# Linear attention on one core: keys turned by VectorE in 32x32 blocks and carried through device memory, in place of turns on TensorE

## What is computed

```python
x = L0_attn_x
n = layernorm(x)
q, k = phi(n @ Wq.T + bq), phi(n @ Wk.T + bk)      # phi = elu + 1, 16 heads of 32
v = n @ Wv.T + bv
# for each token t, with sums over the tokens up to t of the same sequence:
kv = sum(k[s] outer v[s]);  ksum = sum(k[s])
o[t] = (q[t] @ kv) / (q[t] . ksum + 1e-6)
x = x + o @ Wo.T + bo
x = x + experts(layernorm(x))                      # kept only where counts <= cap
```

## Time and profile before

| | us |
|---|---|
| median of 3 executions | 2012.27 (2009.82 to 2013.5) |
| the profiled execution | 2015.74 |
| its span, first to last instruction | 2013.9 |

### The profile page before, as it was taken

One profiled execution on the slowest core, in us unless ns is written; L12 is line 12 of the kernel. 1 busy time (PEld: TensorE's weight loads), 2 busy tenths in 40 slices (PEclk: granted clock), 3 DMA queues, 4 the chain that ended last, 5 costly groups with the idle time before them and its releaser, 6 DMA issues.

```text
span 2013.9 us, 60872 instructions
## 1 busy us (share of the span) xinstructions
PE 1968.6 (98%) x25932; PEld 1731.4 (86%) x25932; DVE 1524.1 (76%) x3260; ACT 737.3 (37%) x1419; POOL 899.6 (45%) x982
## 2 busy tenths in 40 slices
PE   6899999999999999999999999999999999999997
PEld 5788888888888888888888888888888888888886
DVE  4777777777778877777777877777777797777776
ACT  3333343333433333333333433333333333333332
POOL 3454434545345545345545344544345444355421
PEclk8999999999999999999999999999999999999999
DMA  5221222212222212222212222212222122222111
GB/s 178 64 74 65 85 77 94 86 58 82 85 75 94 87 44 90 91 75 91 90 44 85 90 81 85 77 63 85 84 87 86 59 80 86 75 95 86 44 38 49
DMA packets 87391, 159.28 MB, mean 79 GB/s; under 512 B 15313, under 2 KB 15313, under 8 KB 87121
## 3 DMA queue, kind: packets, MB, share of 16 engines
q1 hardware_dynamic: 84720, 154.83, 22.8%
q10 hardware_dynamic: 2400, 0.55, 0.1%
HBM read 121.66 MB, written 33.68 MB: 77 GB/s over the span
## 4 chain that ended last, share of the span: by engine, by line
PE 91%; DVE 6%; issue 1%; ACT 1%; POOL 1%; DMA 0%; SPq 0%; DVEq 0%; POOLq 0%
PE ring L598 35%; PE ring L612 33%; PE num_ps L700 6%; PE ring L663 6%; PE num_ps L686 3%; PE ring L674 3%; PE num_ps L712 2%; DVE s_mask L867 2%; DVE den L1104 1%; PE ring L635 1%; PE ring L648 1%; DVE rden L1111 1%; DVE v_tok L897 1%; DVE o_lo L1100 1%; ACT o_hi L834 0%
## 5 line engine op out<-in xcount | busy, mean ns | idle before, releaser
L1180 POOL TENSOR_TENSOR k_sum<-k_sum,q_raw 128x512 f32<-128x512 f32 x128 | 164.6, 1286 | 596.2 <-DVE q_raw L878 596.2
L780 ACT ACTIVATE e_tmp<-ring,bias_n 128x512 f32<-128x512 f32 x256 | 176.1, 688 | 396.7 <-PE ring L598 396.7
L867 DVE TENSOR_TENSOR s_mask<-ring,causal 128x512 f32<-128x512 f32 x512 | 315.1, 678 | 0.0
L612 PE MATMUL ring<-wv_hi,xt_hi 128*128 128x260 f32 x1024 | 301.0, 294 | 3.1 <-DVE gate_x L899 2.3
L612 PE MATMUL ring<-wo_hi,o_hi 128*128 128x260 f32 x1024 | 288.2, 281 | 3.2 <-DVE o_lo L1100 1.9
L612 PE MATMUL ring<-wo_hi,o_lo 128*128 128x260 f32 x1024 | 290.7, 284 | 0.0
L612 PE MATMUL ring<-wv_hi,xt_lo 128*128 128x260 f32 x1024 | 289.1, 282 | 0.0
L612 PE MATMUL ring<-wv_lo,xt_hi 128*128 128x260 f32 x1024 | 288.9, 282 | 0.0
L612 PE MATMUL ring<-wo_lo,o_hi 128*128 128x260 f32 x1024 | 288.7, 282 | 0.0
L878 DVE SCALAR_TENSOR_TENSOR k_t<-ring,bias,e_tmp 128x512 f32<-128x512 f32 x128 | 96.2, 751 | 197.1 <-ACT e_tmp L782 194.3
L598 PE MATMUL ring<-xt_hi,wk_hi 128*128 128x512 f32 x512 | 215.8, 421 | 7.4 <-DVE wk_lo L322 5.6
(11 more groups left out here) (145 smaller groups left out, 4211.3 us busy)
## 6 DMA issues: line engine op xcount, KB each, us to landing
x_tok<-in_x SPq DMA_DIRECT2D x128, 256.0 KB, 3.8
res<-in_x SPq DMA_DIRECT2D x128, 256.0 KB, 2.7
out<-res SPq DMA_DIRECT2D x128, 256.0 KB, 2.0
x_in<-in_x_t SPq DMA_DIRECT2D x124, 256.0 KB, 4.6
x_rows<-moments_rows SPq DMA_DIRECT2D x31, 512.0 KB, 3.7
k_t<-in_wk_t SPq DMA_DIRECT2D x1, 1024.0 KB, 9.7
q_raw<-in_wq_t SPq DMA_DIRECT2D x1, 1024.0 KB, 11.8
v_tok<-in_wv_t SPq DMA_DIRECT2D x1, 1024.0 KB, 13.9
```

The costliest lines, as they stand in the source:

```text
L612: mm = pe.matmul(bank[:, 0:HW], rows[a](k), w[b][:, k, h, :], start=n == 0, stop=n == 3 * KD - 1)
L780: act.activation(e_tmp[:, m], bank, ACT.Relu, bias=bias_n[:, m, g:g + 1], scale=-1.0).then_inc(phi_relu.handle, 1)
L867: dve.tensor_tensor(s_mask[:, j], ring[:, st.bank(u)].rearrange("p (g t) -> p g t", g=KD), repeat(causal, KD), ALU.mult).then_inc(free[st. ...
L1180: pool.tensor_tensor(k_sum[:, g], k_sum[:, g], q_raw[:, g], ALU.mult).then_inc(prod.handle, 1)
```

## The change

The four transposes on PE and the copy by ACT go. DVE turns a tile's keys with one instruction that transposes each 32x32 block in place of its own (`turn_keys`, now in DVE's program) into a new buffer `k_turned`. The blocks still have to change places between groups of 32 partitions: SP writes `k_turned` (256 KB) to a buffer in device memory (`send_keys`) and reads it back with four transfers, one for each 32 partitions of the target (`fetch_keys`), in pieces of 128 elements, into one of two buffers `k_tok`. PE's `add_state` waits for the four. Tile 1's keys are turned at the start of tile 0 in DVE's order, tile 2's at the start of tile 1, tile 3's at c = 2 behind the chunk V0, and tile 0's of the next block at c = 3 behind `xt_lo` of tiles 0 and 1; each in front of that tile's phi or `o_lo`. The last tile of every second block isn't turned any more, because its state isn't used; before it was.

The ring loses its four "T" uses, so a block has 48 places in place of 54. The constant `spread` is made smaller, to find room, and is set by four copies on 32 partitions in place of one.

```diff
-SKIPS = {0: 1, 1: 1, 3: 3}
+SKIPS = {0: 1, 3: 2}
...
-        uses += [("T", c)] + chunk_uses(c, 0, 1)
+        uses += chunk_uses(c, 0, 1)
...
+        def send_keys(b, c):
+            if (b, c) not in KEY_TILES:
+                return
+            n = KEY_TILES.index((b, c))
+            sp.wait_ge(keys_turned.handle, n + 1)
+            if n > 1:
+                sp.wait_ge(keys_in[n % 2].handle, 16 * HPG * (n // 2))
+            sp.dma_start(keys_dram[n % 2], k_turned).then_inc(keys_out.handle, 16)
+
+        def fetch_keys(b, c):
+            if (b, c) not in KEY_TILES:
+                return
+            n = KEY_TILES.index((b, c))
+            sp.wait_ge(keys_out.handle, 16 * (n + 1))
+            if n > 1:
+                before, tile = KEY_TILES[n - 2]
+                sp.wait_ge(summed.handle, TPB * before + tile + 1)
+            heads = keys_dram[n % 2].rearrange("(i a) j x -> j a i x", i=HPG)
+            for j in range(HPG):
+                sp.dma_start(k_tok[j * HD:(j + 1) * HD, n % 2].rearrange("a i g b -> a i (g b)"), heads[j]
+                             ).then_inc(keys_in[n % 2].handle, 16)
...
-                if c == 0 and st.has("turn"):
-                    load_x(st)
-                    load_features(st)
+                if c == 0:
+                    send_keys(t, 1)
+                    if st.has("turn"):
+                        load_x(st)
+                    fetch_keys(t, 1)
+                    if st.has("turn"):
+                        load_features(st)
+                if c == 1:
+                    send_keys(t, 2)
...
+                if c == 1:
+                    fetch_keys(t, 2)
+                if c == 2:
+                    send_keys(t, 3)
+                    fetch_keys(t, 3)
+                if last and st.has("proj"):
+                    send_keys(t + 1, 0)
+                    fetch_keys(t + 1, 0)
...
-            for g in range(KD):
-                mm = pe.transpose(bank[:, g * P:(g + 1) * P], k_t[:, st.off % 2, g, c * P:(c + 1) * P], ident)
-            mm.then_inc(full[st.bank(u)].handle, 1)
...
-            pe.wait_ge(free[st.bank(("T", c))].handle, st.freed(("T", c)))
+            n = KEY_TILES.index((st.off, c))
+            pe.wait_ge(keys_in[n % 2].handle, 16 * HPG * (n // 2 + 1))
...
-                if attn:
-                    u = ("T", c)
-                    act.wait_ge(full[st.bank(u)].handle, st.filled(u))
-                    act.activation(k_tok, ring[:, st.bank(u)], ACT.Copy).then_inc(free[st.bank(u)].handle, 1)
...
+        def turn_keys(b, c):
+            if (b, c) not in KEY_TILES:
+                return
+            n = KEY_TILES.index((b, c))
+            if n:
+                dve.wait_ge(keys_out.handle, 16 * n)
+            dve.transpose(k_turned.rearrange("p j (g b) -> p g j b", g=KD),
+                          k_t[:, b % 2, :, c * P:(c + 1) * P].rearrange("p g (j a) -> p g j a", j=HPG)
+                          ).then_inc(keys_turned.handle, 1)
...
+                if c < 2 and attn:
+                    turn_keys(st.off, c + 1)
...
+                if c == 2 and attn:
+                    turn_keys(st.off, 3)
+                if last and proj:
+                    turn_keys(st.off + 1, 0)
```

More of the change, by code:

```diff
@@ L76, in ring_uses_alone @@
 def ring_uses_alone():
-    uses = [("T", 0)]
+    uses = []
     for c in range(TPB):
         if c < TPB - 1:
-            uses += scores_of(c + 1) + [("T", c + 1)]
+            uses += scores_of(c + 1)
         uses += [("O", (c, 0)), ("O", (c, 1))]
@@ L88 @@
 BANK_ALONE = {**{("S", (c, j)): j for c in range(1, TPB) for j in range(HPG)},
-              **{("T", c): HPG for c in range(TPB)},
-              **{("O", (c, h)): HPG + 1 - h for c in range(TPB) for h in range(2)}}
+              **{("O", (c, h)): HPG + h for c in range(TPB) for h in range(2)}}
 assert len(USES) % NBANK == 0
@@ L96, in part_of @@
         return "proj" if place[0] == 0 else "attn"
-    return "attn" if kind in ("T", "O") else "proj"
+    return "attn" if kind == "O" else "proj"
 def uses_of(parts):
@@ L184, in attention @@
     moments_dram = nc.dram_tensor("moments_rows", (2, P, TPB, 2), F32, kind="Internal").ap()
+    keys_dram = nc.dram_tensor("keys_turned", (2, P, TPB, P), F32, kind="Internal").ap()
+    KEY_TILES = [(b, c) for b in range(n_blocks) for c in range(TPB) if b % 2 == 0 or c < TPB - 1]
     out_t = io["out"].rearrange("(n p) d -> n p d", p=P)
@@ L227, in attention @@
     head_cols = sb("head_cols", [P, 2, HD])
-    spread = sb("spread", [P, 2, KD, P], F32R)
+    spread = sb("spread", [P, 2, P], F32R)
     bias = sb("bias", [P, 2, KD])
@@ L340, in set_from_constants @@
         dve.wait_ge(const_set.handle, CONSTS)
-        dve.tensor_copy(spread, spread_f).then_inc(bias_set.handle, 1)
+        for g in range(KD):
+            rows = slice(g * HD, (g + 1) * HD)
+            dve.tensor_copy(spread[rows], spread_f[rows, :, g]).then_inc(bias_set.handle, 1)
         dve.tensor_reduce(lo_rows, low.rearrange("p s g j -> p (s g j)"), AXX, ALU.add
                           ).then_inc(bias_set.handle, 1)
-        dve.wait_ge(bias_set.handle, BIASES + 2)
+        dve.wait_ge(bias_set.handle, BIASES + KD + 1)
     def set_gates(dve):
@@ L435, in attention @@
     summed = sem("summed")
+    keys_turned, keys_out = sem("keys_turned"), sem("keys_out")
+    keys_in = [sem(f"keys_in{n}") for n in range(2)]
     kv_summed, kv_kept = sem("kv_summed"), sem("kv_kept")
@@ L647, in spread_reciprocals @@
                     k, rows = BANK[("R", g)], slice(g * HD, (g + 1) * HD)
-                    mm = pe.matmul(ring[:, k, s * BT // 2:(s + 1) * BT // 2], spread[rows, s, g, :], rden[rows],
+                    mm = pe.matmul(ring[:, k, s * BT // 2:(s + 1) * BT // 2], spread[rows, s], rden[rows],
                                    start=True, stop=True, skip_group_check=True, tile_position=(g * HD, 0))
@@ L711, in add_state @@
                     cols = slice((g * HPG + j) * HD, (g * HPG + j + 1) * HD)
-                    pe.matmul(kv_ps[j * HD:(j + 1) * HD, g * HD:(g + 1) * HD], k_tok[:, cols], v_tok[:, c, cols],
+                    pe.matmul(kv_ps[j * HD:(j + 1) * HD, g * HD:(g + 1) * HD], k_tok[:, n % 2, j, g], v_tok[:, c, cols],
                                    start=first_tile(st, c) and g == 0, stop=g == KD - 1, skip_group_check=True,
@@ L723, in body @@
                 last = c == TPB - 1
-                if attn and (proj or c == 0):
-                    turn_keys(st, c)
                 if c == 1 and not attn:
@@ L749, in body @@
                     chunks(st, c, 2, 3)
-                if not proj and not last:
-                    turn_keys(st, c + 1)
                 if attn:
```

11 lines of the change are left out of this document (5 added, 6 removed).

## The result

The changed kernel takes 1964.09 us (median of four executions, 1961.08 to 1965.99); the kernel before, in executions beside it, 2012.88. The ratio is 0.9757 [0.9739, 0.9776]: 48.8 us less, where 51.1 were forecast; the median lies in the range, 1952 to 1985, and in the likelier 1954 to 1968. The profiled execution took 1966.0 us (span 1964.2), where the sum gave 1964.6.

A forecast was written before the change was run, and what follows sets the result against it. PE's distances from start to start were taken to bound all blocks but first and last. -52.0 saved on PE, +0.6 and +0.3 at the start give -51.1: 1961.2 us median, range 1952 to 1985, likely 1954 to 1968.

The forecast's parts named there:

- PE saves per block: Four sets of transposes and three changes of matmul kind leave PE: 0.42 + 0.43 + 0.43 + 0.41 = 1.69 us.
- DVE's transpose: Each new 128x512 transpose on DVE takes 0.69 us, like the statistics instruction; range 0.35 to 3.4.
- slack before the block's first K matmul: DVE's last `xt_lo` of tile 3 ends at 996.74, PE is free for K matmuls at 997.26: 0.52 us.
- a transpose at which the pace of before returns: In tile 3 a DVE transpose of 1.28 + 1.69 = 3.0 us uses up the whole gain per block.
- slack of tile 0's keys: Store, four loads and landing take 8.8 us of a 12.0 us budget before `add_state`: 3.2 us left.
- The first half of the question: What the turns cost PE, as distances from start to start: 1.69 us per block, 52.4 over 31 blocks.
- the prediction's 52.0: PE's whole saving: 52.4 us over 31 blocks, less 0.4 at the first block's tile 0, where PE waits for DVE.
- Rival (C): PE is bound by something unseen, such as weight loading; the freed 1.7 us per block become wider distances: 2012; chance 0.03.
- Rival (A): DVE's transpose is slow, tile 3's pace passes to DVE from 1.28 us; chance 0.05 for 1970 to 2005, 0.05 slower.
- The keys' way: Tile 0's keys through memory: store 0.3 and 2.0, four issues 1.86, landing 4.6, together 8.8 us; hidden, costing nothing.
- The end: Last block: two tiles wait for keys, against ACT's copy leaving the chain; between -2 and +4 us, taken as 0.
- The start: First block, where DVE sets the pace: one transpose adds 0.6 us, setting `spread` by four copies adds 0.3.

The follow-up runs named there:

- double: The kernel before with each of its four transposes per tile issued twice on PE, 512 more in all: 2065.37 us, ratio 1.0263.
- t3_plus3: The changed kernel with DVE's transpose of tile 0's keys, in tile 3 ahead of `o_lo`, issued four times: 2023.03 us, ratio 1.0048.
- t3_plus1: The changed kernel with DVE's transpose of tile 0's keys, in tile 3 ahead of `o_lo`, issued twice: 1974.12 us, ratio 0.98.
- trip2: The changed kernel with two more 256 KB stores, each waited for, on SP ahead of the loads of tile 0's keys: 1968.75 us, ratio 0.9773.
- no_keys: The changed kernel with keys turned, sent and fetched for the first two tiles only, later tiles using those old keys: 1956.59 us, ratio 0.9713.
- tail_early: The changed kernel with the last block's keys of tiles 1 and 2 turned, sent and fetched one tile earlier: 1959.53 us, ratio 0.9729.
- trip4: The changed kernel with four more 256 KB stores, each waited for, on SP ahead of the loads of tile 0's keys: 2100.69 us, ratio 1.0457.

## Why the prediction was right, and where it was not

| step | forecast, us | measured, us |
|---|---|---|
| PE saves per block | 1.69 | 1.77 |
| PE's saving in the stretch | 30 x 1.69 + 0.42 = 51.1 | 30 x 1.77 + 0.3 = 53.4 |
| irregular waits in the stretch | no change | +1.2 |
| the stretch | -51.1 | -52.1 |
| DVE's transpose | 0.69 | 0.692 |
| slack before the block's first K matmul | 0.52 + 0.07 = 0.59 | 0.56 |
| a transpose at which the pace of before returns | 3.0 | 2.93 |
| landing of the loads of tile 0's keys | 4.6 | 2.0 |
| slack of tile 0's keys | 3.2 | 5.2 |
| start | +0.9 | +1.7 and 0.0 |
| end, with PE's saving there | -0.8 | +0.7 and +1.6 |

**The bound.** PE set the pace before and sets it after. The first half of the question, what the removed work costs PE, was read from distances of starts, and a block without the sets is shorter by that, 1.77 where 1.69 were read. The prediction's starts "0.09 apart" are a set's 0.35 divided by four; they are 0.108 apart but for the last. For whole sets this changes nothing, but it made the expectation for double too low. Of the 0.08 above my 1.69, 0.03 to 0.05 stand between K0 and K2, where I had 0.42 and the shortest distances give 0.45 and 0.47 for the two kinds of block; the rest is spread over the other three places. 30 blocks of 1.77 are 53.1, the way from the first K0 to the first K2 gave 0.3, the irregular waits took 1.2: 52.2, against 52.1 measured. That this is the prediction's 52.0 is chance in part: the 52.0 cover 0.8 us that lie behind the stretch, and blocks that saved more paid for waits that nobody had forecast. Rival (C) falls with this: the freed time didn't turn up as wider distances.

**The transpose** took 0.692 us, as the nearest row (the statistics) had it, not the copy below nor the reciprocal above. Rival (A) had its place, its point of entry and its slope right, but each late start costs some 0.1 us more than the wait, and t3_plus3 shows a first victim that I hadn't looked for, the mask of scores in front of tile 3's output matmuls. On whether the kernel gains, the pace answers at 2.93 us; with the waits that vary, the total loses the gain sooner. Between t3_plus1 (0.7 us more, +10.0) and t3_plus3 (2.24 more, +58.9) a straight line reaches 48.8 at about 1.9 us more, so at a transpose of 2.6: interpolated, not run.

**The keys' way** was priced too dearly in one term. I took the landing of x by features, 4.6 us, for the four loads; they land in 2.0. Timeline of SP after, at tile 0's keys, and of PE where they are read:

```profile
1027.42 0.32 SPq L543 DMA_DIRECT2D keys_turned<-k_turned  x1
1029.43 1.74 SPq L555 DMA_DIRECT2D k_tok<-keys_turned  x4
```

```profile
1038.45 0.46 PE L748 MATMUL num_ps<-v_tok,k_tok 128*32 128x32 f32 x32
```

The last load is issued at 1031.2 and lands at about 1033.2; 5.2 us are left, in place of 3.2. Nothing of the result hung on it, which trip2 confirms. A median hides two things here. The last load of tile 1's keys takes 4.6 us in the median and up to 6.6, behind the loads of x; it has over 9 us of slack. And tile 3's keys have no more slack than tile 0's: in the kernel after 5.2 us in the median and 2.6 in the worst block, where tile 0's have 4.4 in the worst but the last.

**The end** is the term that was furthest off, though it lay inside its own bounds. I set the loss of two waiting tiles against the gain of the copy by ACT and took 0, beside the 0.8 us that PE saves there. The gain is there: no_keys, without the keys' transfers and transposes, takes 81.8 us, 3.0 less than before. The waits eat it, and more: timeline of PE in the last block after, then SP's row of the store that came late, and the windows that follow PE's wait:

```profile
1930.93 0.46 PE L748 MATMUL num_ps<-v_tok,k_tok 128*32 128x32 f32 x32 [1.76 <-DMA k_tok<-keys_turned]
...
1939.90 0.46 PE L748 MATMUL num_ps<-v_tok,k_tok 128*32 128x32 f32 x32 [1.19 <-DMA k_tok<-keys_turned]
```

```profile
1923.44 0.34 SPq L543 DMA_DIRECT2D keys_turned<-k_turned  x1
1927.59 1.74 SPq L555 DMA_DIRECT2D k_tok<-keys_turned  x4
```

```profile
1930.00:1931.00 1.00, 0.07 (x7) 0.07 (x11) 0.93 (x4) 0.26 (x1) 0.00 (x0) 1.00 0.74 140
...
1932.00:1933.00 1.00, 1.00 (x24) 0.62 (x16) 0.00 (x0) 0.00 (x0) 0.62 (x1) 0.50 0.93 328
```

Two waits make 3.0 us, the store took over 4 us to land in place of 2.0, and behind the first wait the granted clock is 0.50 for some 3.4 us, which cost up to 1.7. tail_early, which undoes the waits, gets back 2.8 and 3.7 us of it.

**The start** isn't settled. Forecast were +0.9; the two executions of the kernel after show +1.7 and 0.0, and kernels with the same beginning spread over 3.4 us. An effect of that size can't be seen there.

**Irregular waits** weren't in the sum. They are 7.3 us before, and 7.4 to 8.5 after, with another make-up: before, all waits of PE that the profile shows in the stretch stood at the reciprocals spread over rows, after, partly there and partly at `xt_lo`, of whose slack the transpose has left 0.56 us. In the kernel after most of them go with POOL's addition; in the kernel before the rows point the same way, and no run tests it.

**The rules weighed.** The 275 ns of the Trainium skill ("TensorE: Matmul & The Clock Gate", Part 4: PE-mode transpose) are the duration that a row shows, and not what a transpose adds in a dense row of matmuls, 0.11 us here. The rule that puts 128x128 transposes on TensorE ("VectorE: DVE Perf Modes", Rules for kernel authors) didn't hold for this kernel: PE set the pace, DVE had a hole, and the longer way through memory was 2.4% faster.

## What to carry to other kernels

Where one engine sets the pace, work taken from it is worth the distance between starts that it leaves behind, and work given to another costs nothing as long as it fits into a named hole and whatever stands behind that hole has slack; measure both by the row, and the break-even can be told before the run. Here the way through device memory cost nothing in steady state and some microseconds in the last block, where less work covers it; start it a tile earlier there. A wait of PE can cost more than its length: here 0.1 us in the restart, and behind 19 of 30 waits of 1.6 to 4.4 us a stretch at half the clock.

## What the runs showed of the hardware

- Single stores took far longer than usual: 7 of the 112 stores of keys in the kernel after over 4 us to land, up to 5.2, where 2.0 is the median (one of them, 4.15 us to the next step, made PE wait in the last block), and one of moments 3.35 in place of 1.42.
- DVE instructions with two sources in SBUF that begin beside an instruction of POOL last longer, to one undisturbed length behind POOL's end: `xt_lo` up to 3.04 us for two quarters in place of 1.29, the scans 1478 ns in the mean in place of 1286. The 32x32 transpose, with one source, doesn't: 692 ns either way.
- In a set of four or eight float32 transposes PE's starts are 0.108 us apart, and the next matmul starts 0.03 behind the last, though a row gives each 274 to 277 ns.
- PE's granted clock fell to 0.50, 1.2 GHz, for 3.4 us, right after PE had gone back to work behind a wait (1.96 us in trip4, 1.76 in the last block of the kernel after). The second wait of that block, 1.19 us, was not followed by it, and in trip4 neither were 11 of 30 waits of 1.6 us and more.
- A K matmul that starts behind a wait or a busy row of another kind takes about 0.1 us more until the next one starts; this comes on top of every wait.
